# Delta stage of a two-expert hybrid block: whole levels, VectorE's work dealt anew over the slots, three convolution taps behind the state

## The reference

```
q, k, v = silu(causal_conv4(x @ W{q,k,v}) + bias)       # 16 heads of 128, 4 taps
g    = -exp(A_log) * softplus(x @ Wfa @ Wfb + dt_bias)  # decay, per channel
beta = sigmoid(x @ Wb)
q, k = l2norm(q) * 128**-0.5, l2norm(k)
step: S = S * exp(g); vd = (v - S^T k) * beta; S = S + k vd^T; o = S^T q
out  = rmsnorm(o) * o_norm_w * sigmoid(x @ Wga @ Wgb) @ Wo
```

## Time and profile before

| | |
|---|---|
| median of 3 runs | 3721.74 us (3715.66 to 3722.37) |
| the profiled execution | 3717.97 us, its span 3715.8 us |
| mean granted TensorE clock | 0.965 of full speed |
| TensorE matmul busy over the span | 3474.6 us (94%) |
| VectorE busy | 1941.4 us (52%) |
| ScalarE busy | 1427.4 us (38%) |
| GpSimd busy | 125.0 us (3%) |

### The profile page before, as it was taken

How to read it: one execution, slowest core, us unless ns; L and a number is a source line. 1 busy time by engine, 2 the same in 40 slices (tenths; PEclk the granted TensorE clock), 3 DMA queues, 4 the chain that set the end, 5 groups by cost and what they waited for, 6 DMA issues and landing times. The chain is left out here.

```text
span 3715.8 us, 86134 instructions
## 1 busy us (share of the span) xinstructions
PE 3474.6 (94%) x37416; PEld 1694.5 (46%) x37416; DVE 1941.4 (52%) x3334; ACT 1427.4 (38%) x3313; POOL 125.0 (3%) x457
## 2 busy tenths in 40 slices
PE   6979999996789999999999999999999759999999
PEld 4454444442344544444444444444444435444444
DVE  2131111113778897789878878887888431111111
ACT  1010000001466656666665666566656521000000
POOL 0000000000000000000000000000000000000000
PEclk9979999997989999999999999999999868999999
DMA  4011100003111111121111111111211042000000
GB/s 154 7 57 36 28 0 29 11 0 120 48 31 36 42 50 34 45 66 41 33 56 43 48 50 45 42 37 39 65 39 34 16 154 63 14 15 29 0 12 12
DMA packets 83725, 156.21 MB, mean 42 GB/s; under 512 B 8782, under 2 KB 33998, under 8 KB 79516
## 3 DMA queue, kind: packets, MB, share of 16 engines
q1 hardware_dynamic: 83356, 150.77, 12.3%
HBM read 133.71 MB, written 17.04 MB: 41 GB/s over the span
## 5 line engine op out<-in xcount | busy, mean ns | idle before, releaser
L1333 PE MATMUL psum<-dl_xt,dl_wqkv 128*128 128x512 f32 x1536 | 778.2, 624 | 10.4 <-DVE dl_qkv L977 10.0
L513 DVE SCALAR_TENSOR_TENSOR f_act_g<-psum,f_bup,f_act_g 128x512 f32<-128x512 f32 x96 | 72.1, 751 | 939.4 <-ACT f_act_g L468 939.4
L977 DVE SCALAR_TENSOR_TENSOR dl_qkv<-psum,dl_par,dl_qkv 128x511 f32<-128x511 f32 (+2 forms) x576 | 430.4, 747 | 14.0
L468 ACT ACTIVATE f_act_g<-psum,f_bgate 128x512 f32<-128x512 f32 x96 | 66.0, 687 | 923.1 <-PE psum L411 923.1
L1333 PEld LDWEIGHTS psum<-dl_xt,dl_wqkv 128*128 128x128 f32 x1536 | 257.4, 189 | 250.2 <-issue 212.5
L411 PE MATMUL psum<-xnt_sb,wup 128*128 128x512 f32 x768 | 345.2, 592 | 0.0
L407 PE MATMUL psum<-xnt_sb,wgate 128*128 128x512 f32 x768 | 345.2, 592 | 0.0
L429 PE MATMUL psum<-f_wdown,f_hidden 128*128 128x512 f32 x768 | 344.9, 592 | 0.0
L1340 PE MATMUL psum<-dl_wo,dl_sg 128*128 128x512 f32 x512 | 260.9, 623 | 2.9 <-DVE dl_qkv L977 2.5
L407 PEld LDWEIGHTS psum<-xnt_sb,wgate 128*128 128x128 f32 x768 | 145.9, 190 | 183.7 <-issue 183.7
L411 PEld LDWEIGHTS psum<-xnt_sb,wup 128*128 128x128 f32 x768 | 145.9, 190 | 183.7 <-issue 183.7
(11 more groups left out here) (192 smaller groups left out, 4618.1 us busy)
## 6 DMA issues: line engine op xcount, KB each, us to landing
dl_wqkv<-in_dw_qkv SPq DMA_DIRECT2D x192, 256.0 KB, 2.6
dl_wo<-in_dwo SPq DMA_DIRECT2D x16, 1024.0 KB, 5.2
f_weights_b<-f_weights_by_expert SPq DMA_DIRECT2D x48, 256.0 KB, 6.3
wgate<-in_wgate SPq DMA_DIRECT2D x2, 3072.0 KB, 18.6
wup<-in_wup SPq DMA_DIRECT2D x2, 3072.0 KB, 24.7
f_wdown<-in_wdown SPq DMA_DIRECT2D x2, 3072.0 KB, 13.6
x_sb<-in_x SPq DMA_DIRECT2D x4, 1024.0 KB, 9.3
x_after_experts<-x_sb SPq DMA_DIRECT2D x16, 256.0 KB, 2.0
```

What stands on the lines that cost most here:

```text
L977: tap_ = lambda dl: dve.scalar_tensor_tensor(y_[:, dl:TT], ps[:, bank, 0:TT - dl], par[:, h, 4 * a + 3 - dl:4 * a + 4 - dl], y_[:, dl:TT], ...
L1333: last = pe.matmul(ps[:, bank, :], wq[:, n % RING, m, :], xt[:, u // HG % 2, m, :], start=(m == 0), stop=(m == KC - 1))
```

## The change

Five edits of the delta stage, in one:

1. Levels are whole. `level_scale` multiplies late queries and keys of all 512 tokens in one instruction and early keys in one; `level_decay` joins the decays in one. TensorE makes each level in one piece.
2. VectorE's list is dealt anew. In slots 7 to 11 `level_scale` stands ahead of `add_state`, `level_decay` and `level_take` behind it, in the slot after the product. Rows, `o_scale`, `decayed`, `norm_tables`, `blocks_out` (now slot 12, behind the state) and `blocks_in` (now slot 14, ahead of it) move too.
3. All three taps of a projection stand behind `add_state`.
4. The three boundary columns of a quarter of the unit's projections are added in one instruction for four heads (`edges`), once all four are convolved, and silu waits for it (`edged`). The boundary has two buffers.
5. The series has three terms (one 2048-wide step fewer), its limit is 2^-8 in place of 2^-6, and the comparison comes last and signals `series_done`.

```diff
-             (6, "states"): [("level", w, 0, first)], (6, "inner"): [("level", w, 0, second)],
-             (6, "split"): [("level", w, 1, first)], (6, "end"): [("level", w, 1, second)],
-             (8, "end"): [("sums", w, 0, every)],
+             (6, "inner"): [("level", w, 0, quarters)], (6, "end"): [("level", w, 1, quarters)],
+             (8, "inner"): [("sums", w, 0, every)],
...
-             (14, "inner"): [("cross", w, 0, first), ("krow", w, 2, every)], (14, "end"): [("cross", w, 0, second)],
-             (15, "inner"): [("vrow", w, 0, every), ("corner", w, 0, first)], (15, "end"): [("corner", w, 0, second)]}
+             (14, "inner"): [("krow", w, 2, every)], (14, "end"): [("cross", w, 0, quarters)],
+             (15, "inner"): [("vrow", w, 0, every)], (15, "end"): [("corner", w, 0, quarters)]}
...
-    if 7 <= sl <= 10 and at in ("inner", "end"):
-        jobs.append(("level", w, sl - 5, first if at == "inner" else second))
+    if 7 <= sl <= 10 and at == "end":
+        jobs.append(("level", w, sl - 5, quarters))
...
+                def edges(u, a):
+                    dve.wait_ge(s["bnd_ready"], u + 1)
+                    for j in range(HJ):
+                        wait_read(dve, "proj", u, 4 * (1, 0, 2)[a] + j)
+                    dve.tensor_tensor(qkv[:, a, :, 0:3], qkv[:, a, :, 0:3], bnd(u)[:, a], ALU.add).then_inc(s["edged"], 1)
...
+                def level_scale(u, lv):
+                    m, nb, kk_, dv = cut(u, lv)
+                    wait_full(dve, "level", u, lv)
...
+                    o.done(dve.tensor_tensor(late, late, dv[:, :, 0, 0:1].unsqueeze(1).broadcast_to([P, 2, nb, m]), ALU.mult))
+                    dve.tensor_tensor(kk_[:, :, 0, :], kk_[:, :, 0, :], dv[:, :, 1, 0:1].broadcast_to([P, nb, m]),
                                       ALU.mult).then_inc(s["late"], 1)
+                def level_decay(u, lv):
+                    m, nb, kk_, dv = cut(u, lv)
+                    dve.wait_ge(s["late"], LEVELS * u + lv)
+                    o.done(dve.tensor_tensor(dv[:, :, 0, 0:1], dv[:, :, 0, 0:1], dv[:, :, 1, 0:1], ALU.mult))
...
+                            level_scale(w, sl - 6)
+                        if prep and sl == 0:
+                            series(w, 0)
+                        if prep and sl == 1:
+                            series(w, 2)
+                        if prep and sl == 3:
+                            softplus(w)
+                        if post and sl == 4:
+                            o_scale(p, 2)
+                            o_scale(p, 3)
...
+                        if prep and sl in (5, 6):
+                            decayed(w, (QQ, KK)[sl - 5])
+                        if prep and sl == 12:
+                            norm_tables(w)
...
+                        if prep and sl == 14:
+                            blocks_in(w)
 
                         if run:
                             add_state(k, sl)
                         if post and sl in (4, 5):
                             gated(p, 2 * sl - 8)
                         if conv:
+                            convolve(*conv, False)
                             convolve(*conv, True)
+                        if prep and sl in (0, 4, 12):
+                            edges(w, {0: QQ, 4: KK, 12: VV}[sl])
+                        if before and before[0] == "rows":
+                            add_rows(*before[1:])
+                        if prep and sl == 0:
+                            series(w, 1)
+                        if prep and sl == 1:
+                            near_zero(w)
+                        if prep and sl == 2:
+                            choose(w)
...
+                        if prep and 7 <= sl <= 11:
+                            level_decay(w, sl - 6)
+                            level_take(w, sl - 6)
...
+                        if prep and sl == 11:
+                            whole_decay(w)
+                        if prep and sl == 12:
+                            blocks_out(w)
```

More of the change, by code:

```diff
@@ L547, in short_jobs @@
     w, w2, p = k + 1, k + 2, k - 1
-    every, first, second = None, (0, 1), (2, 3)
+    every, quarters = None, (0, 1, 2, 3)
     table = {(0, "inner"): [("krow", k, 3, every), ("vrow", k, 1, every)],
@@ L825, in silu @@
                 def silu(u, a, signal):
-                    for j in range(HJ):
-                        wait_read(act, "proj", u, 4 * (1, 0, 2)[a] + j)
+                    act.wait_ge(s["edged"], 3 * u + (2, 1, 3)[a])
                     act.activation(qkv[:, a], qkv[:, a], ACT.Silu).then_inc(signal, 1)
@@ L980, in convolve @@
                     if not late:
-                        if i == 0:
-                            dve.wait_ge(s["bnd_ready"], u + 1)
                         dve.wait_ge(s["tapped"], 12 * u + i + 1)
-                        step(dve.tensor_tensor(y_[:, 0:3], y_[:, 0:3], bnd[:, a, j, :], ALU.add))
                         step(tap_(1))
@@ L997, in boundary @@
                         dve.wait_ge(s["tapped"], 12 * (u - HG) + 12)
-                    o.done(dve.tensor_tensor(bnd[:], tl, taps(0, 3), ALU.mult))
+                    o.done(dve.tensor_tensor(bnd(u), tl, taps(0, 3), ALU.mult))
                     step(dve.tensor_tensor(bnt[:, :, :, 0:2], tl[:, :, :, 1:3], taps(1, 2), ALU.mult))
-                    step(dve.tensor_tensor(bnd[:, :, :, 0:2], bnd[:, :, :, 0:2], bnt[:, :, :, 0:2], ALU.add))
+                    step(dve.tensor_tensor(bnd(u)[:, :, :, 0:2], bnd(u)[:, :, :, 0:2], bnt[:, :, :, 0:2], ALU.add))
                     step(dve.tensor_tensor(bnt[:, :, :, 0:1], tl[:, :, :, 2:3], taps(2, 1), ALU.mult))
-                    dve.tensor_tensor(bnd[:, :, :, 0:1], bnd[:, :, :, 0:1], bnt[:, :, :, 0:1],
+                    dve.tensor_tensor(bnd(u)[:, :, :, 0:1], bnd(u)[:, :, :, 0:1], bnt[:, :, :, 0:1],
                                       ALU.add).then_inc(s["bnd_ready"], 1)
@@ L1023, in near_zero @@
                         dve.wait_ge(s["o_ps"], SLOTS * (u - 1))
-                    o.done(dve.tensor_scalar(flat(kq(u)[:, 1]), flat(sg[:]), 2.0 ** -6, None, ALU.is_lt))
-                    mark[("near", u)] = o.n
+                    o.wait(mark[("series", u, 2)])
+                    dve.tensor_scalar(flat(kq(u)[:, 1]), flat(sg[:]), 2.0 ** -8, None, ALU.is_lt).then_inc(s["series_done"], 1)
                 def choose(u):
                     ln, mask = flat(kq(u)[:, 0]), flat(kq(u)[:, 1])
-                    o.wait(mark[("near", u)])
+                    o.wait(mark[("series", u, 2)])
                     dve.wait_ge(s["series_done"], u + 1)
@@ L1365, in block_part @@
                             pe.wait_ge(s["decayed"], 2 * u + 2)
-                    if kind == "level" and n > 1 and quarter % 2 == 0:
-                        pe.wait_ge(s["late"], 2 * (LEVELS * u + n - 2) + quarter // 2 + 1)
+                    if kind == "level" and n > 1 and quarter == 0:
+                        pe.wait_ge(s["late"], LEVELS * u + n - 1)
                     for g in range(4 * quarter, 4 * quarter + 4):
@@ L1384, in block_part @@
                                                  start=True, stop=True)
-                    if kind == "level" and quarter == 1:
-                        last.then_inc(s["half_level"], 1)
                     if quarter == 3:
```

106 lines of the change are left out of this document (28 added, 78 removed).

## The result

The changed kernel takes 3924.26 us (median of 4 runs, 3920.40 to 3933.61) against 3718.70 us before: a ratio of 1.056, 95% interval 1.053 to 1.058. The profiled execution took 3923.93 us. The direction was forecast; the size was not: +205 us where +119 was predicted, and the time lies above the range.

The account below looks back on a forecast made before the run. TensorE's own list was taken to bound the kernel, busy 1714.91 of 1774.00 us. Added waits of +112, start-up -4 and clock +11 gave 119 on the profiled 3717.97 us, with the median 3.8 above: 3841 us, range 3775 to 3900.

Parts of the forecast that it names:

- slot 1: TensorE's wait for the residual, forecast to grow from 0.80 to 1.35 us as more VectorE work precedes it.
- slots 3 and 4: Next main job waits for a convolved projection's bank, freed behind three taps after the state: 0.35 us each.
- slots 5 and 6: Main jobs wait for the last tap, as `gated` and the state stand ahead of the taps: 1.33 us each.
- slot 8: Level 3 waits for level 2's bank, copied out behind state, rows and `level_decay`: 1.9 us.
- slot 11: First `dec` waits for level 5's bank, copied out behind state, three taps and decay: 3.0 us, the largest term.
- slot 13: Residual waits because `blocks_out` joins three taps behind slot 12's state: 0.8 us.
- slots 14 and 15: `blocks_in` ahead of slot 14's state makes it late; `cross` waits 0.95, the next main job 0.5: 1.45 us.
- slot 12's 1.25: Old wait for the residual, forecast to go because `blocks_out` leaves the stretch ahead of it: 1.25 us.
- The count of 14 units: 13 units have all added waits, the first with a recurrence and the fifteenth half each: 14 x 8.0 = 112.
- half of them: 13 x 1.7/2 = +11: Clock term: half of slot 11's 13 waits of 3.0 us bring a half-clock stretch costing 1.7 us: +11.
- Rival (a): Each of a unit's three longest waits brings a half-clock stretch: 71 in place of 11, total 3900; chance 0.13.
- the -4 us of the start-up unit: VectorE's saved work in the start-up unit, where TensorE waits for VectorE, gives 0 to 8 us; -4 taken.

Follow-up runs that it names:

- e1: Changed kernel with the copy out of level 5's bank in slot 11 ahead of the addition of the state: 3874.65 us, ratio 1.042.
- e10: Kernel before with, in slot 11 only, taps 1 and 2 behind the state and level 5's copy behind all three taps: 3768.37 us, ratio 1.013.
- e3: Changed kernel with copies of levels 1 to 5 ahead of the state and each level in two runs, one main step between: 3868.32 us, ratio 1.040.
- e4: e3 with taps 1 and 2 ahead of the state in most slots, blocks_out ahead of slot 12's state and other moves: 3751.50 us, ratio 1.008.
- e5: e4 with TensorE's order alone changed: two main steps between level halves in slots 7, 9, 10, cross and corner in halves: 3756.42 us, ratio 1.010.
- e6: e5 with level 5's level_decay and whole_decay ahead of slot 11's state, ga and fa behind the state step: 3725.55 us, ratio 1.002.
- e8: Kernel before, levels in halves, TensorE's order nearly kept, plus the change's series, one-instruction boundary columns and several placements: 3698.28 us, ratio 0.994.

## Why the prediction was wrong

**Right: the bound and the waits.** The kernel is bound by TensorE's list, and VectorE's saved work bought nothing. The waits forecast slot by slot, against the means over the 13 units: slot 1 1.35 and 1.35; slots 3 and 4 0.35 each, and 0.27 each; slots 5 and 6 1.33 each, and 1.06 and 1.35; slot 8 1.9 and 1.87; slot 11 3.0 and 2.83; slot 13 0.8 and 0.87; slots 14 and 15 1.45 and 1.20; slot 12's 1.25 is gone. Slot 5's mean is low because three of the 13 units have `beta` at the end of slot 4 and no wait behind it; the other ten wait 1.38. In sum +8.0 us per unit forecast, +7.3 measured. The count of 14 units was right too: the first with a recurrence grew by 5.7 us and the fifteenth by 10.0, together one more unit. `level_decay` on 512 columns, every fourth one, the price that no row showed, took 1.08 us (1.1 was taken):

```profile
L1066 DVE TENSOR_TENSOR dl_dec<-dl_dec 128x512 f32<-128x512 f32 x16 | 17.4, 1084 | 0.0
```

The Trainium skill (VectorE: DVE Perf Modes, the section on the TRN2 errata) gives (N+151)/0.96 ns for a four-byte addition of N columns, 0.69 us for 512, and has no term for a stride. The trace agrees for the half of level 1, every second column of 512, with 0.70 us on average before the change; for every fourth column it does not.

**Wrong, first: "half of them: 13 x 1.7/2 = +11".** The term was mis-sized. At 13 of the 14 waits of `dec` between 1116 and 3090 us a half-clock stretch began within some 1.3 us of the wait's end, not at half of them (the expectation for e1 counted 12), and some of these stretches lasted 6.8 us and not 3.4. Of the 23 stretches in the 13 units 12 are of this kind; seven began at or shortly behind `cross` and four at idle times of the new kind elsewhere. Together 3.81 us per unit, 53 us in 14. e1 takes the wait out and 16 of 23 stretches go; e10 puts it into the kernel before and 10 come. Rival (a) named this mechanism with 71 us; the slot 8 wait of 1.9 us, which it counted too, brought none by itself.

**Wrong, second: the sum has no term for what whole levels do to TensorE's supply of instructions.** The step costed the levels on VectorE alone and took a level issued in one piece to cost TensorE what its halves did. It cost 3.5 us per unit, 49 us in 14, and some of the half clock besides. The rows that could have warned stood in the trace: the windows view counts 59688 records of matmuls and loads, the DMA queues 237 fetches of 16 KB.

**Wrong, third, small:** the -4 us of the start-up unit: the first residual starts at 1051.6 us against 1051.5 us before, so nothing was won. The account closes, with 14 units for each term as in the forecast: 119, less 10 (waits, 7.3 in place of 8.0), plus 42 (clock, 14 x 3.81 less 11), plus 49 (14 x 3.47 without a releaser), plus 4 is 204 of 205 us.

What stays open: what decides whether an idle time is followed by a half-clock stretch. Waits of 2.8 us were at 13 of 14 in the changed kernel and at 10 of 13 in e10; those of 1.75 us in slot 8 were not, while behind `cross` three stretches began with idle times of 0.88 and 0.53 us alone. Open too is why e3, e4, e5 and e6, which share TensorE's levels in two runs behind the state step, have 122.4 to 122.6 us per unit as a remainder, where the kernel before has 121.2 (the expectation for e8 has 121.2 us for "every kernel so far"; only the others come near it).

## What to carry to other kernels

Before an instruction of the second engine is moved behind another, ask for each bank which it frees who claims it next and when; done slot by slot from one timeline, this gave every wait here within 0.3 us. A long wait of TensorE can have a second price: here 7.3 us of added waits per unit came with 3.8 us of half clock, so look for such stretches behind like waits and give them a term of their own. And when many tiny products are put in one row, count instructions against the fetches in the DMA view: merging helps the engine that computes with one long instruction and can starve the one that computes with hundreds of short ones.

## What the runs showed of the hardware

- TensorE can run out of instructions: a 16 KB fetch serves some 252 records, and the idle times end 2.2 to 3.0 us behind the start of one. 256 records in 1.3 us (a whole level) or in some 2.3 us (halves with one step between) can starve it; spread over some 3.2 us they mostly don't (2.08 to 0.53 us per unit, e4 to e5). Both spreads are estimates, from 0.65 us for a half and 0.96 us for a main step.
- One idle time of 2.83 us is mostly followed by 3.4 us, sometimes 6.8, at a granted clock of 0.50 (1.2 GHz of 2.4), a loss of 1.7 or 3.4 us, although TensorE was about 90% busy in the steady part. The Trainium skill (TensorE: Matmul & The Clock Gate, the section on depth-cycling of the PSUM queue) tells of the like behind short idle times between groups; in this trace the waits of 1.35 us in slots 5 and 6 brought none, and those of 1.75 us in slot 8 neither.
- VectorE's product of 512 four-byte columns in SBUF took 0.70 us when it took every second column and 1.08 us when it took every fourth (lines `L1071` before and `L1066` after, means of 32 and 16).
